# Moving the own-chunk normalization into the loop over the previous chunks

## The reference

```python
x = x + attn(layernorm(x))      # z = ln(x) @ W.T; four gated scans m over the rows,
                                # h = z + sum_k eta_k m_k; output gamma * layernorm(h) + beta
x = x + ffn(layernorm(x))       # Hadamard transform, up and gate (2048 x 8192), silu(gate) * up,
                                # Hadamard transform, down (8192 x 2048)
```

## Time and profile before

| what | us |
|---|---|
| median of 2 runs | 6813.87 (6810.63 to 6817.11) |
| profiled execution, its own time | 6809.56 |
| its span on the slowest core (core 4) | 6808.0 |
| span of the other cores | 6749.3 to 6798.1 |

### The profile page before, as it was taken

The page is one execution under the profiler, slowest core; times in us unless marked ns, Lnnn a source line. Parts: engine busy times, 40 slices in busy tenths (PEclk is TensorE's granted clock), DMA queues, the critical chain, the costliest instruction groups (busy, mean ns, idle before and its releaser), DMA issues.

```text
span 6808.0 us, 49985 instructions; the slowest of 8 cores (6749.3 to 6808.0 us)
## 1 busy us (share of the span) xinstructions
PE 3481.7 (51%) x16269; PEld 1517.6 (22%) x16543; DVE 2382.1 (35%) x2879; ACT 959.1 (14%) x2027; POOL 221.3 (3%) x423
## 2 busy tenths in 40 slices
PE   0000101046661169999999999121112395665844
PEld 0000000012220024444444444000000142232311
DVE  5666311124445621111111111345533533232322
ACT  3444111111112230000000000121112000000000
POOL 0000100000000000000000000000000010010100
PEclk9999955567665569999999999555555698887977
DMA  3555899961211112211211111211131464545553
GB/s 62 87 84 86 123 130 129 128 96 50 62 50 56 44 44 59 59 56 56 59 56 56 56 56 44 77 50 49 50 97 51 114 180 112 162 124 147 142 143 88
DMA packets 413912, 574.27 MB, mean 84 GB/s; under 512 B 34201, under 2 KB 329693, under 8 KB 403421
## 3 DMA queue, kind: packets, MB, share of 16 engines
q1 hardware_dynamic: 355710, 403.25, 20.4%
q0 software_dynamic: 57952, 167.81, 17.9%
HBM read 638.05 MB, written 167.77 MB: 118 GB/s over the span
## 4 chain that ended last, share of the span: by engine, by line
PE 45%; DVE 24%; DMA 9%; issue 7%; another core or an unknown queue 6%; ACT 5%; SPq 4%; DVEq 1%; ACTq 0%; POOL 0%; POOLq 0%
PE pd L1131 13%; PE pu L902 13%; PE pg L909 13%; DMA ep<-x_dram 4%; DVE statc L405 4%; DVE vq L999 3%; DVE btmp L997 3%; PE pz L634 2%; SPq L968 2%; DVE vq L1001 2%; ACT vq L981 1%; PE pq L977 1%; DMA x_dram<-hb 1%; SPq L1016 1%
## 5 line engine op out<-in xcount | busy, mean ns | idle before, releaser
L1131 PE MATMUL pd<-wdsl,v2sl 128*128 128x512 bf16 x4014 | 897.1, 383 | 431.7 <-DMA v2sl<-v_dram 356.1
L902 PE MATMUL pu<-uT_s,wslab 128*128 128x512 bf16 x4014 | 901.5, 380 | 5.1 <-ACT uT_s L851 0.8
L909 PE MATMUL pg<-uT_s,gslab 128*128 128x512 bf16 x4014 | 899.8, 379 | 4.3
L924 DVE SCALAR_TENSOR_TENSOR vtmp<-pu,wsupT,silb 128x1024 f32<-128x1024 f32 x128 | 164.3, 1284 | 1550.5 <-ACT silb L918 1550.5
L977 PE MATMUL pq<-vq,h_s 128*128 128x256 bf16 x512 | 183.3, 372 | 847.0 <-DMA vq<-v_dram 761.6
L1131 PEld LDWEIGHTS pd<-wdsl,v2sl 128*128 128x128 bf16 x4096 | 401.7, 99 | 927.1 <-issue 459.0
L1139 DVE TENSOR_TENSOR acc<-acc,pd 128x512 f32<-128x512 f32 x512 | 352.3, 688 | 640.3 <-PE pd L1131 640.3
L902 PEld LDWEIGHTS pu<-uT_s,wslab 128*128 128x128 bf16 x4096 | 400.8, 98 | 485.9 <-issue 3.5
L909 PEld LDWEIGHTS pg<-uT_s,gslab 128*128 128x128 bf16 x4096 | 401.1, 98 | 483.0
L997 DVE TENSOR_TENSOR btmp<-vq 128x8192 bf16<-128x8192 bf16 x48 | 212.4, 4425 | 551.1 <-ACT vq L981 546.9
L462 PE MATMUL pp<-w4b,xlnT_s 128*128 128x4 bf16 x1792 | 63.4, 166 | 665.9 <-DVE xlnT_s L451 665.9
(11 more groups left out here) (145 smaller groups left out, 2136.1 us busy)
## 6 DMA issues: line engine op xcount, KB each, us to landing
v2sl<-v_dram SPq DMA_DIRECT2D x256, 512.0 KB, 11.5
xlnT_s<-xfull POOLq DMA_DIRECT2D x112, 512.0 KB, 6.1
wup_bf<-wupT POOLq DMA_DIRECT2D x16, 2048.0 KB, 215.3
wgate_bf<-wgateT POOLq DMA_DIRECT2D x16, 2048.0 KB, 539.3
G<-xown SPq DMA_DIRECT2D x32, 1024.0 KB, 33.7
wslab<-wup_bf SPq DMA_DIRECT2D x512, 64.0 KB, 2.2
gslab<-wgate_bf SPq DMA_DIRECT2D x512, 64.0 KB, 2.2
v_dram<-vchB SPq DMA_DIRECT2D x64, 512.0 KB, 2.7
```

What stands on the lines that cost most here:

```text
L902: last = pe.matmul(pu[par][:, s * 512:(s + 1) * 512], wslab[w % 2][:, c * 256 + jj * 128: c * 256 + (jj + 1) * 128], uT_s[:, c * T + hh * ...
L909: last = pe.matmul(pg[par][:, s * 512:(s + 1) * 512], gslab[w % 2][:, c * 256 + jj * 128: c * 256 + (jj + 1) * 128], uT_s[:, c * T + hh * ...
L924: m_stt_prev = DV.emit(lambda dv, jc=jc, par=par: dv.scalar_tensor_tensor(vtmp2[:, :], pu[par][:, :], wsupT[:, jc:jc + 1], silb2[:, :], AL ...
L1131: last = pe.matmul(pd[par][:, :], v2sl[sp_][:, jj * T + tch * 128: jj * T + (tch + 1) * 128], wdsl[sp_][:, jj * 512:(jj + 1) * 512], start ...
```

## The change

The a0 loop becomes a function emit_a0_chunk(j), the prep loop a function emit_prep_chunk(jp), and they are written out interleaved: after every seventh prep chunk comes one a0 chunk. Since a0 writes xlnT_s while prep still runs, prep's ring (three loaded slots, two slots of centred rows) moves to wzT_s. The W load goes into wzT_s, so GpSimd now waits for the end of prep and a0 on PE, ACT and DVE before it issues it; the up and gate copies stand behind it as before. The G loads of a0 no longer wait for the end of marow. What an a0 chunk and a prep chunk execute is unchanged.

```diff
-        for jp in range(PREV):
+        def emit_prep_chunk(jp):
...
             GPX3[b3].emit(lambda gp, jp=jp, b3=b3: gp.dma_start(
-                out=xlnT_s[:, b3 * D:(b3 + 1) * D],
+                out=wzT_s[:, b3 * D:(b3 + 1) * D],
                 in_=xfull[jp * 128:(jp + 1) * 128, :]))
...
+        def emit_a0_chunk(j):
+            b = j % 2
+            if j >= 2:
+                SY.wait(AC, m_a0_ac[j - 2])
+            m_ld = SYG[b].emit(lambda sy, j=j, b=b: sy.dma_start(
+                out=G[b][:, :], in_=xown[j * 128:(j + 1) * 128, :]))
...
+        for _k in range(PREV):
+            emit_prep_chunk(_k)
+            if _k % 7 == 6:
+                emit_a0_chunk(_k // 7)
+        m_prep_end_dv = DV.n
+        m_prep_end_ac = AC.n
+        m_prep_end_pe = PE.n
+
+        GP.wait(PE, m_prep_end_pe)
+        GP.wait(AC, m_prep_end_ac)
+        GP.wait(DV, m_prep_end_dv)
         for c in range(DC):
             GPZ.emit(lambda gp, c=c: gp.dma_start(
                 out=wzT_s[:, c * D:(c + 1) * D], in_=wzT[c * 128:(c + 1) * 128, :]))
...
-        for j in range(TC):
-            b = j % 2
-            SY.wait(AC, m_prep_end_ac)
-            SY.wait(DV, m_prep_end_dv)
-            if j >= 2:
-                SY.wait(AC, m_a0_ac[j - 2])
```

More of the change, by code:

```diff
@@ L387, in build_nc @@
         m_prep_pe = []
-        for jp in range(PREV):
+        m_a0_ac = []
+        m_a0_pe = []
+        m_a0_norm = []
+        m_prep_end_dv = 0
+        m_prep_end_ac = 0
+        m_prep_end_pe = 0
+        slot_user = [0] * 2
+        def emit_prep_chunk(jp):
             b3 = jp % 3
@@ L405, in build_nc @@
             DV.emit(lambda dv, b3=b3, sp=sp: dv.reduce_sum(
-                statc[:, sp:sp + 1], xlnT_s[:, b3 * D:(b3 + 1) * D], axis=AX.X))
+                statc[:, sp:sp + 1], wzT_s[:, b3 * D:(b3 + 1) * D], axis=AX.X))
             DV.wait(DV, DV.n)
@@ L414, in build_nc @@
             mss = AC.emit(lambda ac, b3=b3, sp=sp: ac.activation(
-                zbf[:, :], xlnT_s[:, b3 * D:(b3 + 1) * D], AF.Square,
+                zbf[:, :], wzT_s[:, b3 * D:(b3 + 1) * D], AF.Square,
                 accum_out=statc[:, sp + 2:sp + 3]))
@@ L451, in build_nc @@
             mcast = DV.emit(lambda dv, b3=b3, b=b, sp=sp: dv.tensor_scalar(
-                xlnT_s[:, (3 + b) * D:(4 + b) * D],
-                xlnT_s[:, b3 * D:(b3 + 1) * D],
+                wzT_s[:, (3 + b) * D:(4 + b) * D],
+                wzT_s[:, b3 * D:(b3 + 1) * D],
                 statc[:, sp + 1:sp + 2], None, ALU.add))
@@ L462, in pmm @@
                     last = pe.matmul(pp2[:, 4 * c:4 * c + 4],
-                                     xlnT_s[:, xc0 + c * 128: xc0 + (c + 1) * 128],
+                                     wzT_s[:, xc0 + c * 128: xc0 + (c + 1) * 128],
                                      w4b[b][:, :],
@@ L469, in build_nc @@
             m_prep_pe.append(m_pe)
+        def emit_a0_chunk(j):
[4 more added lines that the diff above has]
+                out=G[b][:, :], in_=xown[j * 128:(j + 1) * 128, :]))
+            DV.wait(SYG[b], m_ld)
+            DV.emit(lambda dv, b=b: dv.reduce_sum(statc[:, 0:1], G[b][:, :], axis=AX.X))
+            DV.wait(DV, DV.n)
+            DV.emit(lambda dv: dv.tensor_scalar_mul(statc[:, 1:2], statc[:, 0:1], -1.0 / D))
+            mdn = DV.n
+            AC.wait(DV, mdn)
+            msq = AC.emit(lambda ac, b=b: ac.activation(G2h[:, :], G[b][:, 0:1024], AF.Square))
+            DV.wait(AC, msq)
+            mr0 = DV.emit(lambda dv: dv.reduce_sum(statc[:, 2:3], G2h[:, :], axis=AX.X))
+            AC.wait(DV, mr0)
+            msq2 = AC.emit(lambda ac, b=b: ac.activation(G2h[:, :], G[b][:, 1024:2048], AF.Square))
+            DV.wait(AC, msq2)
+            DV.emit(lambda dv: dv.reduce_sum(statc[:, 6:7], G2h[:, :], axis=AX.X))
+            DV.wait(DV, DV.n)
+            DV.emit(lambda dv: dv.tensor_add(statc[:, 2:3], statc[:, 2:3], statc[:, 6:7]))
+            DV.wait(DV, DV.n)
+            DV.emit(lambda dv: dv.tensor_scalar_mul(statc[:, 3:4], statc[:, 2:3], 1.0 / D))
+            DV.emit(lambda dv: dv.tensor_mul(statc[:, 5:6], statc[:, 1:2], statc[:, 1:2]))
+            DV.wait(DV, DV.n)
+            mvar = DV.emit(lambda dv: dv.tensor_sub(statc[:, 3:4], statc[:, 3:4], statc[:, 5:6]))
+            AC.wait(DV, mvar)
+            AC.emit(lambda ac: ac.activation(statc[:, 4:5], statc[:, 3:4], AF.Ln,
+                                             bias=consts[:, 0:1]))
+            AC.wait(AC, AC.n)
+            mrs = AC.emit(lambda ac: ac.activation(statc[:, 4:5], statc[:, 4:5], AF.Exp,
+                                                   scale=consts[:, 2:3]))
+            if ka0 < 2:
+                m_a0_ac.append(AC.n)
+                m_a0_pe.append(PE.n)
+                m_a0_norm.append(DV.n)
+                return
+            DV.wait(AC, mrs)
+            if j >= 2:
+                DV.wait(PE, m_a0_pe[j - 2])
+            else:
+                DV.wait(PE, m_prep_end_pe)
+            mnorm = DV.emit(lambda dv, b=b: dv.tensor_scalar(
+                Hh[b][:, :], G[b][:, :], statc[:, 1:2], statc[:, 4:5], ALU.add, ALU.mult))
+            if ka0 < 3:
+                m_a0_ac.append(AC.n)
+                m_a0_pe.append(PE.n)
+                m_a0_norm.append(DV.n)
+                return
+            PE.wait(DV, mnorm)
+            for c in range(DC):
+                slot = c % 2
+                PE.wait(AC, slot_user[slot])
+                mt = PE.emit(lambda pe, b=b, c=c, slot=slot: pe.transpose(
+                    ptA[slot][:, 0:128],
+                    Hh[b][:, c * 128:(c + 1) * 128], i128b_s[:, :]))
+                AC.wait(PE, mt)
+                mcp = AC.emit(lambda ac, c=c, j=j, slot=slot: ac.copy(
+                    xlnT_s[:, c * T + j * 128: c * T + (j + 1) * 128],
+                    ptA[slot][:, 0:128]))
+                slot_user[slot] = mcp
+            m_a0_ac.append(AC.n)
+            m_a0_pe.append(PE.n)
```

## The result

| | before | changed |
|---|---|---|
| median of all runs, us | 6812.93 (12 runs) | 6836.52 (13 runs) |
| ratio | 1 | 1.0029, 95% interval 1.0017 to 1.0041 |
| profiled execution, span of its slowest core, us | 6808.0 (core 4) | 6835.0 (core 5) |

The change moves waits from one stage to another and leaves the time nearly where it was: 0.3% slower, clear of noise. The profiled spans differ by 27 us, the medians by 24, and the ratio gives 20; the sum had 25. The medians include some disturbed runs; the ratio leaves them out.

The account below looks back on a forecast made before the run. Prep bound by a serial DVE/ACT exchange, a0 by DMA traffic of the copies, z by a serial chain; 336 us won before z, given back in z, sum +25 us on 6809.6, median 4.3 higher: 6839 us, range 6745 to 6905.

Parts of the forecast that it names:

- the sum: All terms up to the end of z: last x2 store at 2069.7 against 2044.8 us, so +25 us.
- Step 1: Prep with a0: an inserted a0 chunk costs 16.85 us, its G load hidden; both end at 1026.7 us.
- Step 4: z stage under the copies: the G load decides, 89.8 us a chunk against 37.57 alone; store priced like a load.
- The stated range, 6745 to 6905: Whole-kernel time, to hold 8 in 10, taking in the store-only case and half the way to the period's bounds.
- 6717 and 6889: Whole-kernel times in us if a z chunk beside the copies took 60 or 113 us.
- The fit that step 4 quotes from the Trainium skill: Any DMA transfer: 2.0 us plus bytes over 436 GB/s, 4.4 us for 1 MB; beside the copies, z not slowed.
- A z stage not slowed by the copies: Rival, z stage: 37.57 us a chunk all through, z ends at 1709, total 6478 us; chance 0.07.
- a store at half the load's rate: Rival, z stage: x2 store lands after 81.2 us, a chunk takes 127 us, total 6911 us; chance 0.06.
- the store alone decides: Rival, z stage: only the store is slow, 74.5 us a chunk, total 6784 us; chance 0.13.
- the 336 us: Lead at the start of z, 1103.3 against 1439.33 us, given back by seven chunks at 52 us more.

Follow-up runs that it names:

- the grouped transpositions: Changed kernel with an a0 chunk's transpositions and ACT copies in four groups, each behind the Square of one of the next four prep chunks; ratio to before 0.9905.
- The half-row kernels: Changed kernel and kernel before, each with every up and gate copy cut into two of 128 rows by 4096 columns; ratios to before 0.9753 and 0.9658.
- before, pieces in prep: Kernel before with the up and gate copies cut into 128 pieces of 32 rows, 112 behind prep's loads; profiled 6717.5 us, ratio 0.9836.
- the last kernel: Changed kernel with grouped transpositions and copies in 128 pieces of 64 rows by 4096 columns, 80 in prep, 48 behind z; 6356.4 us, ratio 0.9317.

## Why the prediction was right

| step | forecast | measured |
|---|---|---|
| an a0 chunk inside prep | 16.85 us | 17.1 (587.21 to L427 at 606.81, less the 2.5 of a chunk without) |
| end of prep and a0 | 1026.7 | 1028.9 |
| marow's first matmul | 1083.2 | 1082.7 |
| start of the z stage | 1103.3 | 1103.7 |
| last copy landed | 1743 | 1734.7 (1055.0 + 679.7) |
| x2 store, G load beside the copies | 43.7, 80.6 | 42.4, 78.3 |
| a z chunk beside the copies | 89.8 | 92.7 for the first, then 88.0 |
| eighth x2 store | 1769.1 | 1766.4 |
| a z chunk alone | 37.57 | 37.6 |
| end of z | 2069.7 | 2067.6 |

*Step 1* held with its mechanism: the grouped transpositions took away just the part that was put down to ACT's queue. The G loads in prep were hidden, as assumed (4.9 us to land, issued a chunk ahead).

*Step 4* was the one without a row of its own, the store beside the copies. It is shown twice, by its landing in the changed kernel (42.4) and by the 37.5 us periods when the copies are moved away. That the load and not the store decides was right by 12 us a chunk. Its picture of one row of z waiting for one row of the copies was only nearly right: the packets of the copies held two rows by the counts above, and the 144 and 144 packets of the earlier trace rows include the small ones (3.67 MB are 112 packets of 32 KB, against 128 rows of the load). The price was safe from this, since it was taken from the load's landing and not worked out from packets.

Part of the closeness of the end is luck of small errors that cancel: the store and its load landed 1.3 and 2.3 us sooner than taken, so the seventh x2 store came 7 us early, but the copies ended 8 us early too and left the following chunk at 78.5 us instead of 74.5; z ended 2 us early and what is behind it took 5 us more.

The stated range, 6745 to 6905, does not follow from the two times that it is said to take in, 6717 and 6889. The fit that step 4 quotes from the Trainium skill is given there for transfers issued by GpSimd, and z's are issued by SP; nothing in the sum rests on it.

*The rivals.* A z stage not slowed by the copies, and a store at half the load's rate, are both out by the landings. That the store alone decides is out for this kernel, and became true as soon as the load was issued earlier or the copies had shorter rows.

One thing the forecast had not drawn from its own numbers: it took the 336 us as won and then given back. The half-row kernels show it more plainly. a0's engines need 16.6 us a chunk by themselves and 17.1 inside prep; the change only took the waits for G out of a0 (446 us) and put 360 us more of waits for the store and for G into z.

## What to carry to other kernels

When a stage is slow beside a background transfer, moving the stage away exposes the next one; first price each neighbour by the bytes that it needs per step on its critical chain, and put the transfer beside the stage that has slack for it. Cut a background copy into pieces small enough in rows and in number, and issue them between the loads of a stage bound by its engines. Work put into another stage's loop costs the time that it adds to the shared serial chain, here 10.7 us of the two engines' exchange, and copies queued on one of these engines ahead of an instruction that others wait for came on top, here 6.4 us; break them into groups behind that instruction.

## What the runs showed of the hardware

Two queues shared the DMA engines packet by packet and not by bytes: 144 and 144 packets in the earlier trace rows, with 3.67 and 1.05 MB (without the small ones, by the counts, 112 and 128). The copies' mean packet was 26.2 KB with rows of 8192 elements, 7.3 with 4096 and 3.6 with 2048; by the counts, data packets of 32, 8 and 4 KB. A second 1 MB transfer behind the first took 35.9, 12.4 and 6.8 us, at about the same total rate of both queues (127, 139 and 137 GB/s). The short rows made the copies end 37 and some 75 us later than whole rows.

With nothing beside it, a z chunk comes in two lengths, and the x2 store's landing goes with them: 37.5 us with a store of about 6.1, 35.8 with one of 4.8. In the kernel before, core 4 (the slowest) lands its stores in 5.8/6.1/6.4 us, and core 0 has

```profile
DMA to landing us min/median/max: 4.6/4.8/5.2
```

The cores take one or the other in pairs: only 4 and 5 have the longer one in the profiled execution of the kernel before, 0, 1, 4 and 5 in that of the changed one, all eight in that of "before, pieces in prep", none in the last kernel. Over 15 periods this is 26 us of a core's span, whatever the copies do. What sets it is open; a comparison of two single profiles of this kernel has this much play.
